# Causal attention's tail in a decoder kernel: the residual sum as a unit of its own, three weight splits moved, one wait of the plan dropped

## The reference, cut to what matters

```
h = rms(x, n1_w)                                  # per token
q = rms(heads(h @ wq.T), qn_w); k = rms(heads(h @ wk.T), kn_w); v = heads(h @ wv.T)
attn = softmax(where(causal, q @ k.T * HD**-0.5, -inf))      # 16 heads of 16 channels
ao = (attn @ v) @ wo.T;  ao[:, :, :64] = 0
x = x + ao
xf = rms(x, n2_w)
o0 = gelu(xf @ e0_up.T) @ e0_down.T;  o1 = silu(xf @ e1_w1.T) * (xf @ e1_w2.T) @ e1_down.T   # and o2, o3
x = x + weighted sum of o0..o3 (first 64 channels 0)
```

## Time and profile before

| | |
|---|---|
| median of three runs | 1236.60 us (1233.26 to 1237.04) |
| the profiled execution's own time | 1241.81 us |
| its span, first to last instruction | 1240.0 us |
| busy: TensorE / VectorE / ScalarE / GpSimd | 1033.9 / 659.6 / 588.5 / 281.7 us |
| mean granted clock of TensorE | 0.911 of full speed |
| last product of the cross-attention's heads to the experts' first product | 1026.9 to 1090.4 us |

### The profile page before, as it was taken

How to read it: one execution, slowest core, us unless ns; L and a number is a source line. 1 busy time by engine, 2 the same in 40 slices (tenths; PEclk the granted TensorE clock), 3 DMA queues, 4 the chain that set the end, 5 groups by cost and what they waited for, 6 DMA issues and landing times.

```text
span 1240.0 us, 21582 instructions
## 1 busy us (share of the span) xinstructions
PE 1033.9 (83%) x8592; PEld 733.1 (59%) x8592; DVE 659.6 (53%) x1638; ACT 588.5 (47%) x1392; POOL 281.7 (23%) x285
## 2 busy tenths in 40 slices
PE   7986788887857776779999878989888888779996
PEld 4664466664457774445666666767666665446654
DVE  3254556567637763244454556777767674535103
ACT  5532365552355552334454444555556544564642
POOL 2511132001500003221112110312322023233543
PEclk9997689898879998889999997999999888678998
DMA  9351345105656833542225224323123005000001
GB/s 303 90 87 46 77 111 130 30 11 169 192 195 227 332 114 115 155 131 72 91 76 174 75 75 132 101 80 96 46 80 100 25 2 212 1 1 1 1 1 31
DMA packets 67398, 123.69 MB, mean 100 GB/s; under 512 B 11569, under 2 KB 43025, under 8 KB 63217
## 3 DMA queue, kind: packets, MB, share of 16 engines
q1 hardware_dynamic: 64528, 117.48, 31.1%
q0 software_dynamic: 1536, 3.67, 0.9%
q10 hardware_dynamic: 1232, 1.15, 0.3%
HBM read 86.30 MB, written 35.92 MB: 99 GB/s over the span
## 4 chain that ended last, share of the span: by engine, by line
PE 60%; DVE 19%; ACT 10%; POOL 3%; issue 3%; DMA 3%; SPq 1%; DVEq 0%; POOLq 0%; ACTq 0%
PE psum L393 43%; DVE s_p L2626 2%; ACT s_p L2584 2%; POOL rs L2916 2%; PE psum L1333 2%; PE psum L2543 2%; DVE s_max L2615 2%; PE psum L2554 2%; PE psum L1305 1%; PE psum L2715 1%; DVE s_pT L2607 1%; DVE s_max L1445 1%; DVE wu L1284 1%; DVE wd L1284 1%; PE psum L1321 1%
## 5 line engine op out<-in xcount | busy, mean ns | idle before, releaser
L2584 ACT ACTIVATE s_p<-psum,s_max 112x375 f32<-112x375 f32 x128 | 72.3, 570 | 87.7 <-DVE s_max L2615 87.7
L660 POOL TENSOR_TENSOR rstd<-meanvar,minus_half 112x1 f32<-112x1 f32 x40 | 22.8, 570 | 282.6 <-DVE meanvar L629 230.1
L1445 DVE TENSOR_REDUCE s_max<-psum 112x2 f32<-112x750 f32 x64 | 59.3, 935 | 30.0 <-PE psum L1305 28.9
L393 PE MATMUL psum<-Wv,ctx 128*125 128x512 f16 x240 | 62.9, 422 | 13.0 <-issue 10.0
L2916 POOL TENSOR_TENSOR rs<-ms,minus_half 112x32 f32<-112x32 f32 x8 | 43.5, 5442 | 110.3 <-DVE ms L2850 110.3
L393 PE MATMUL psum<-ctx,Wk 128*128 128x375 f16 x320 | 62.3, 330 | 5.0 <-ACT s_yT L2173 2.8
L2543 PE MATMUL psum<-ident,s_p 112*125 112x112 f32 x384 | 61.6, 295 | 3.9 <-DVE s_p L2626 2.3
L2615 DVE TENSOR_REDUCE s_max<-psum 112x1 f32<-112x375 f32 x128 | 63.7, 540 | 2.3 <-PE psum L2535 2.1
L608 ACT ACTIVATE s_v<-psum 125x512 f32<-125x512 f32 x48 | 28.6, 597 | 75.4 <-PE psum L393 45.8
L1395 ACT ACTIVATE s_pT<-psum 125x672 f32<-125x672 f32 x64 | 46.7, 731 | 31.2 <-PE psum L1321 29.7
L593 ACT ACTIVATE s_k<-psum 128x375 f16<-128x375 f32 x64 | 31.3, 489 | 62.6 <-PE psum L393 59.0
(11 more groups left out here) (357 smaller groups left out, 2517.2 us busy)
## 6 DMA issues: line engine op xcount, KB each, us to landing
keys<-s_k SPq DMA_DIRECT2D x64, 187.5 KB, 2.3
s_k<-keys SPq DMA_DIRECT2D x8, 1500.0 KB, 8.2
values<-s_v SPq DMA_DIRECT2D x48, 224.0 KB
s_v<-values SPq DMA_DIRECT2D x16, 672.0 KB
raw_wg<-in_wg SPq DMA_DIRECT2D x8, 1024.0 KB
raw_wu<-in_wu SPq DMA_DIRECT2D x8, 1024.0 KB, 5.4
raw_wd<-in_wd SPq DMA_DIRECT2D x8, 1024.0 KB, 5.4
s_kd<-k_halves SPq DMA_DIRECT2D x48, 93.8 KB, 3.8
```

The lines of the kernel that those rows point to most:

```text
L393: ins = TE.matmul(bank, left, right, start=i == 0, stop=last)
L1445: VE.tensor_reduce(s1_max[b % 2][:, 2 * p:2 * p + 2], rings["s1"][unit][0:N, :, 0:S], X, ALU.max, negate=True).then_inc(*V.up("max1", n))
L2584: SC.activation(rings["p4"][2 * n + j], rings["s4"][(n, j)][0:N, 0:S], ACT.Exp, bias=s4_max[b % 2][:, h:h + 1], accum_out=s4_sum[b % 2][:, ...
```

## The change

`wo5` keeps the product on TensorE, and VectorE's sum becomes a unit `wo5e` of its own, placed half a `REST` (750 ns of costs) later; `wo5` now asks for a free bank first, and its bank stays taken in the plan until `wo5e` is placed. The stream `s5_split` is gone: its three splits are placed by the last batch's operands stream, right after `ms5 7`. The condition that `qk5 7` comes only after `pT5 6 1` is dropped.

```diff
-    step("wo5", "T wo5, V xadd5", "misc5", "V xadd5", 640)
+    step("wo5", "T wo5", "misc5", "V xadd5", 640)
+    step("wo5e", "V xadd5")
@@ s5_operands
         yield [("ms5", b)]
+        if b == B - 1:
+            for name in ("e0_up", "e1_w1", "e1_w2"):
+                yield split5(w16_m, name)
         yield from rest(5500.0)
-        if b == B - 1:
-            yield from until(("pT5", b - 1, 1))
         yield [("qk5", b)]
@@ s5_out
         yield from rest(REST)
+        yield from until_banks(1)
         yield [("wo5", b)]
+        yield from rest(REST / 2)
+        yield [("wo5e", b)]
         yield from rest(REST / 2)
         yield [("sqb5", b)]
@@ stream removed
-    def s5_split():
-        yield from until(("qkT5e", B - 1))
-        yield split5(w16_m, "e0_up")
-        yield from until(("s5e", B - 1, 3))
-        yield split5(w16_m, "e1_w1")
-        yield split5(w16_m, "e1_w2")
@@ vector_s5
-        elif what == "wo5":
+        elif what == "wo5e":
             dve.wait_ge(T["wo5", b], V["x", 4, b], G["xin5", b])
-            VE.tensor_tensor(x_tok[:, b, 64:], x_tok[:, b, 64:], ring[unit][0:N, 0:KEPT],
+            VE.tensor_tensor(x_tok[:, b, 64:], x_tok[:, b, 64:], ring[("wo5", b)][0:N, 0:KEPT],
                              ALU.add).then_inc(*V.up("xadd5", b))
```

More of the change, by code:

```diff
@@ L2359, in build @@
     UNITS5 = ("ones5", "rms5a", "ms5a", "qkv5", "qkv5e", "ms5", "qk5", "qkT5", "qkT5e", "s5", "mx5", "s5e", "pT5", "av5",
-              "oT5", "turn5", "atT5", "atT5e", "wo5", "sqb5", "msb5", "xf5", "xfT5", "xfT5e", "split5")
+              "oT5", "turn5", "atT5", "atT5e", "wo5", "wo5e", "sqb5", "msb5", "xf5", "xfT5", "xfT5e", "split5")
     w16 = {}
@@ L2517, in build @@
           follow(s5_operands, range(0, B, 2)), follow(s5_operands, range(1, B, 2)), s5_heads(), follow(s5_out, range(0, B, 2)),
-          follow(s5_out, range(1, B, 2)),
-          s5_split())
+          follow(s5_out, range(1, B, 2)))
     end_stage()
```

## The result

| | before | after |
|---|---|---|
| median of the runs | 1234.93 us (1230.79 to 1237.04, 4 runs) | 1248.64 us (1245.12 to 1253.97, 4 runs) |
| ratio after to before | | 1.0095, interval 1.0051 to 1.0140 |
| the profiled execution's own time, span | 1241.81, 1240.0 us | 1245.12, 1243.3 us |
| busy: TensorE / VectorE / ScalarE / GpSimd | 1033.9 / 659.6 / 588.5 / 281.7 us | 1032.8 / 660.7 / 586.3 / 283.3 us |
| mean granted clock of TensorE | 0.911 | 0.910 |

The changed kernel is slower by 0.5 to 1.4%. The forecast was 1233.5 us with a range up to 1239.8: it was wrong. The busy times are the same, so what was lost is idle time or clock. The two profiles show little of it: their executions are 3.3 us apart where the medians are 13.7 apart.

The account below looks back on a forecast made before the run. The cross-attention was taken as close to TensorE's own work, the tail as a chain of waits; -0.8 - 1.5 - 0.9 - 0.6 + 0.7 = -3.1 us gave 1233.5 us, range 1228.0 to 1239.8.

Parts of the forecast that it names:

- The sum as a unit of its own, batches other than 5: Residual sums outside batch 5: 0.8 us gained, bounds 0 and 2.8; the longer-held bank costs nothing, with 1 us either way.
- 2.4 us on either side for the clock: Three product groups in the tail could fall on the other clock level: 2.4 us either way around the summed forecast.
- the first of my two orders: Last batches' plan, walked from the old plan's state: means of batch 7 stand behind mx5 6 0, power starts about as before.
- Removed idle time, batches other than 5: VectorE's idle time ahead of the residual sums outside batch 5: at most 2.8 us removed, 0.8 us taken as gain.
- Batch 5: VectorE's stall at batch 5's residual sum goes, so batch 7's power starts sooner: 1.5 us gained, bounds 0 and 2.7.
- The dropped wait: qk5 7 on VectorE can follow batch 7's power sooner: 0.9 us gained, of at most 1.9.
- a wait in place of the one removed: Rival: qk5 7 placed too early blocks VectorE until the power ends, 3.6 us of stall; +4.2, 1240.8 us; chance 0.13.
- The splits and the port: Tail: 0.6 us gained by one removed split, 0.7 lost by splits outlasting the power's cover, nothing charged for the SBUF port.
- the rival's sum: Port rival: splits wait on VectorE for the power, qk5 7 starts later; +2.7 us gives 1236.2, perhaps 1239; chance 0.04.
- The copy behind the last transposes: Batch 7's last transposes in the tail: their copy should follow within 0.1 us once the e_w split is gone, 0.6 gained.
- The sum of the tail: From last head product to the experts' first product: the stretch was to be 2 to 4 us shorter than 63.6.
- The last falsifier: Stretch up to the end of the last head product, at 1027 us: moving by over 2 us would prove the prediction wrong.

Follow-up runs that it names:

- e11: Against the kernel before: sum its own unit in all batches, planner counting a bank that waits only for the residual sum as free; one run, 1247.59 us.
- e2: Against the kernel before: only the sum as its own unit, bank asked for, in all batches; old wait and splits kept; 1247.65 us, ratio 1.0107.
- e1: The changed kernel unchanged, run on another chip beside the kernel before; 1252.81 us against 1238.48, ratio 1.0129.
- e4: Against the kernel before: the whole change, but the sum its own unit only from batch 5 on; 1237.12 us, ratio 0.9997.
- e5: Against the kernel before: only the sum as its own unit, from batch 5 on; old splits and wait kept; 1227.35 us, ratio 0.9986.
- e8: Against the kernel before: only qkv5 asking for one free bank instead of two, as a control; 1241.10 us, ratio 1.0095.
- e7: Against the kernel before: sum its own unit in all batches, and qkv5 asking for one free bank instead of two; 1227.46 us, ratio 0.9981.
- e12: Against the kernel before: only the condition on pT5 6 1 ahead of qk5 7 dropped; one run, 1243.21 us.
- e3: Against the kernel before: only the three splits behind ms5 7 and the dropped wait, sum in its old unit; 1241.32 us, ratio 1.0044.
- e10: Against the kernel before: sum its own unit from batch 5 on, wait dropped, splits placed behind batch 6's first maximum; 1234.40 us, ratio 0.9979.
- e6: Against the kernel before: sum its own unit from batch 5 on, three splits behind ms5 7, wait kept; 1230.04 us, ratio 0.9991.
- e9: Against the kernel before: wait dropped, three splits placed behind batch 6's first maximum, sum in its old unit; 1237.69 us, ratio 0.9979.

## Why the prediction was wrong

**The step that failed** is the end of "The sum as a unit of its own, batches other than 5": the held bank moves another unit by half a round, "the pair then takes the freed slot: nothing, with 1 us either way". I took a delay of one unit to be local. In a plan placed in order it is not: each later unit is placed from where the one before it stands, and the causal chains moved against the heads from batches 1 and 2 on, with the missed place of `qkv5 2` as the plainest step, though not by that alone (e11). It measured +5.9 us of idle time in the head stretch, in the changed kernel and in e2, and +3.3 us at the same clock in e2 for the unit as a whole. On top came the clock: 16 runs with the unit in all batches and the old two-bank rule (the result's, e1, e2) have a mean of 0.905 to 0.907, where before has 0.913 on the chip of e1 and e2. By the slope that is 6 to 8 us. I had put 2.4 us on either side for the clock, from three product groups of the tail, and no term for the clock of the long stretch. I also walked the planner only through the last batches, from the state of the old plan: the very assumption that failed. The walk was exact there: `qkv5e 7`, `s5 6 0`, `mx5 6 0`, `ms5 7`, the first of my two orders, is that of the new plan.

**What is shown of the cause, and what not.** Shown: the unit brings the loss (e2), in batches 0 to 4 and not after (e4, e5), it is idle time of TensorE spread over many waits, and in the same runs the clock is lower. Not shown: which property of the order is the bad one. The pairs of `qkv5` looked like it, but e8, where these are even, is worse, and e11 with the bank given back gets back less than half. One reading is left that fits every kernel: those whose residual sums come evenly (e7 and the eight with the plan of before) have 25.1 to 27.0 us idle in the head stretch, those where they come unevenly (after, e1, e2, e8, e11) have 29.0 to 35.0. No run changes that alone, and the amount does not follow the gaps: e8's are smaller than the changed kernel's. Nor is the step from order to clock tested: why these plans get a lower clock is open, since e8 has the most idle time and a clock of 0.913.

**Removed idle time, batches other than 5.** The 11.5 us in front of the sum fell to 0.8, as forecast; the gain of 0.8 didn't come, since the waits went to other operations. The bound of 2.8 us was of the wrong thing: VectorE's idle time in front of the sum, while what counts is whether the idle time of TensorE falls, and in the head stretch it rose.

**Batch 5.** Right, as far as e5 tells it, which has the unit in batches 6 and 7 too. The forecast was 1.5 us of at most 2.7; in e5 the power starts 2.5 us sooner, the tail is 1.5 us shorter and the whole 2.2 ± 0.5 at the same clock. The 1.5 was a middle between two orders, and e5 has neither: its means stand ahead of the first maximum. The nearness of the number is luck.

**The dropped wait.** For the edit alone the sign comes out wrong, as far as one run tells: forecast -0.9, measured +1.4 in the tail in e12. The rival "a wait in place of the one removed" described it rightly, 3.6 us of stall named and 4.3 found, 4.8 in e3, where the splits are too. But it priced stall and splits at 3.6 + 3.7 us, as if all of it reached TensorE, and e3 has +1.6 ± 0.8.

**The splits and the port.** Forecast +0.1 in sum, a power lasting 5.44 us and splits 1.22. The splits did last 1.22 us. The power didn't: 6.35 us in the changed kernel, where the first split started 0.17 us ahead of it:

```profile
1057.92 1.22 DVE L2764 SCALAR_TENSOR_TENSOR e_up<-w_e_up,e_up 128x1024 f16<-128x1024 f32 x1
...
1059.60 2.35 DVE L2764 SCALAR_TENSOR_TENSOR e_w<-w_e_w,e_w 128x1024 f16<-128x1024 f32 x2
```

That is +0.9, and +3.2 in e3. I had asked the port question in one direction only, whether a running power stops VectorE, and not whether a running VectorE operation stops a power. (For the port the prediction says "about 2 us worse" in one place and takes 2.7 in the rival's sum.) The copy behind the last transposes came at once (1082.80 against their end at 1082.77), as forecast.

**The sum of the tail.** -1.5 - 0.9 - 0.6 + 0.7 = -2.3 us was forecast without the unit in the other batches. e4, which is just that, has -3.1 ± 0.6 at the same clock, and e10 -2.5 ± 0.6, so the sum of the tail held there. That is partly luck: there the plan happened to put the splits behind the power's start, and where it did not, in e3, the same two edits came out at +1.6 ± 0.8. In the changed kernel itself the tail is 4.7 us shorter, near the 2 to 4 that I named, but for another reason: 3.0 us are work moved ahead of it, and e2, without the two tail edits, has 4.2 of the 4.7. All in all 0.3% of the program was estimated well, with a sign that looks wrong inside it, while 1% came from a sentence that I had not worked out. The last falsifier, "if the stretch up to 1027 moves by more than 2 us", is the one that fired: 9.2 us.

## What to carry to other kernels

When a change touches what a planner places from (a resource held longer, a delay), write out the whole placed order before and after, from the first unit that it touches, ahead of costing any wait; here the part that it was made for was 3 us and the drift 6. Look at the end of each chain as well as at its start. Give such an edit only to the units that need it: here three of eight batches. Read a run beside its own granted clock: two kernels a per cent apart can be one kernel at two clocks, and a stretch is best compared by TensorE's idle time over the same instructions.

## What the runs showed of the hardware that I had not expected

**A power waited for a running split on VectorE, and the splits did not wait for a power.** With a split (two inputs from SBUF) running at its start, GpSimd's power showed 8.61 us (e3) and 6.35 (after and e1), where it takes 5.44 alone; started first, by 1.1 to 1.4 us, it took 5.44 and the splits beside it their 1.22 (e6, e9; also e4). In e3 it waited for all three splits, which stand back to back; in the changed kernel a maximum, which reads PSUM, stands behind the first split, and the power waited for that one alone. In both the power's 5.44 us, counted back from its end, begin 0.14 us ahead of the end of the last split waited for (1050.37, and 1057.92 + 1.22 = 1059.14). The Trainium skill, page "SBUF — State Buffer", section "SBUF: two separate sides", has a VectorE operation with two SBUF inputs hold the shared port pair for its whole length against a GpSimd operation that reads SBUF: the rows of e3 agree. It has GpSimd hold it likewise against VectorE: the rows of e6 and e9 don't, for this power.

**The same program, 9.3 us apart in one stretch.** The changed kernel's head stretch has 31.2 us idle in both of its profiles, and TensorE is busy 193.7 us at 0.95 in the one and 203.0 at 0.91 in the other. Within one kernel 0.01 of mean clock goes with 10 us of time, about 0.8%, as much as the largest difference between kernels at the same clock (e8).
